# Edge stage of a graph layer on one core: 16-bit one-hots stored in interleaved pairs, addresses without a bit mask, 160 columns of zeros instead of 256

## The reference, cut to what matters

```python
def _conv(h, e, src, dst, Wn_l, bn_l, We_l, be_l, Wc_l, bc_l):
    hn = h @ Wn_l + bn_l
    et = e @ We_l + be_l
    m = hn[src] + et
    s = segment_sum(m, dst, num_segments=N_NODES)
    cnt = segment_sum(ones, dst, num_segments=N_NODES)
    agg = s / maximum(cnt, 1.0)[:, None]
    return concatenate([hn, agg], axis=1) @ Wc_l + bc_l
```

## Time and profile before

| | |
|---|---|
| time, median of 3 runs | 385.04 us (384.15 to 385.57) |
| profiled execution, span from first to last instruction | 380.0 us (the page gives no other time of it) |
| PE busy | 341.5 us, 90% |
| DVE busy | 248.8 us, 65% |
| granted TensorE clock, mean of the span | 0.982 |
| share of PE in the chain that ended last | 84% |

### The profile page before, as it was taken

How to read it: one execution, slowest core, us unless ns; L and a number is a source line. 1 busy time by engine, 2 the same in 40 slices (tenths; PEclk the granted TensorE clock), 3 DMA queues, 4 the chain that set the end, 5 groups by cost and what they waited for, 6 DMA issues and landing times.

```text
span 380.0 us, 9574 instructions
## 1 busy us (share of the span) xinstructions
PE 341.5 (90%) x2763; PEld 250.0 (66%) x2763; DVE 248.8 (65%) x659; ACT 150.1 (39%) x469; POOL 130.3 (34%) x243
## 2 busy tenths in 40 slices
PE   0599999999899999999989999999999999999910
PEld 0467777999688788886745566666666665567800
DVE  1647859993343425076798877769879998467640
ACT  1335536410121504113704466544556665444600
POOL 6200000600000000053670355456556666454536
PEclk9999999999999999999999999999999999999975
DMA  7941105830299930000061679999999999999005
GB/s 208 258 115 49 41 10 126 204 110 11 78 392 385 387 144 0 0 3 0 0 223 56 224 293 385 384 387 385 384 361 387 386 383 387 386 383 340 4 1 67
DMA packets 52456, 79.11 MB, mean 208 GB/s; under 512 B 3307, under 2 KB 19895, under 8 KB 52408
## 3 DMA queue, kind: packets, MB, share of 16 engines
q1 hardware_dynamic: 50458, 76.81, 58.2%
q0 software_dynamic: 720, 0.64, 1.5%
q10 hardware_dynamic: 1230, 1.05, 1.0%
HBM read 77.21 MB, written 1.30 MB: 207 GB/s over the span
## 4 chain that ended last, share of the span: by engine, by line
PE 84%; DVE 5%; DMA 3%; issue 2%; POOL 2%; ACT 1%; SPq 1%; POOLq 0%; DVEq 0%; ACTq 0%
PE ps L1280 82%; DMA reg<-in_L_gnn_Wc_dram 3%; PE ps L1283 3%; POOL out_dram L591 1%; DVE reg L1273 1%; DVE reg L910 1%; DVE cols L1142 0%; POOLq L105 0%; SPq L398 0%; DVE reg L1136 0%; DVE colp L1148 0%; ACT reg L620 0%; ACT reg_w L629 0%; POOL reg_w L580 0%; DVE acc L964 0%
## 5 line engine op out<-in xcount | busy, mean ns | idle before, releaser
L1280 PE MATMUL ps<-reg 128*64 128x256 f32 (+5 forms) x1399 | 237.9, 310 | 2.7 <-issue 1.1
L1280 PEld LDWEIGHTS ps<-reg 128*64 128x64 f32 (+5 forms) x1399 | 163.8, 143 | 17.4 <-issue 4.6
L1280 PE MATMUL ps<-reg,reg_w 128*64 (+1 forms) x688 | 154.9, 384 | 1.4 <-issue 1.3
L1280 PEld LDWEIGHTS ps<-reg,reg_w 128*64 128x64 f32 (+1 forms) x688 | 93.6, 138 | 50.6 <-issue 6.3
L580 POOL TENSOR_TENSOR reg_w<-reg_w 128x128 f32 x150 | 76.2, 508 | 78.4 <-ACT reg_w L811 59.9
L1228 DVE SCALAR_TENSOR_TENSOR reg_w<-reg_w,nid,reg 128x128 f32 x167 | 61.7, 373 | 24.9 <-PE ps L1280 19.2
L810 ACT COPY reg_w<-ps 64x128 f32<-64x128 f32 x150 | 39.3, 262 | 62.6 <-PE ps L1280 62.0
L1228 DVE SCALAR_TENSOR_TENSOR reg<-reg_w,reg 128x128 f32 x150 | 60.9, 406 | 0.4 <-issue 0.4
L1280 PE MATMUL ps<-zeros_b 128*128 128x256 bf16 (+1 forms) x231 | 53.5, 301 | 0.7 <-ACT reg L698 0.7
L811 ACT COPY reg_w<-ps 64x128 f32<-64x128 f32 x150 | 39.0, 260 | 3.7
L910 DVE TENSOR_TENSOR reg<-iota,idxH 125x660 bf16<-125x660 f16 (+5 forms) x42 | 38.8, 991 | 0.0
(11 more groups left out here) (252 smaller groups left out, 292.9 us busy)
## 6 DMA issues: line engine op xcount, KB each, us to landing
reg<-in_L_ffn_w2s_dram SPq DMA_DIRECT2D x127, 512.0 KB, 11.4
reg<-in_edge_attr_dram SPq DMA_DIRECT2D x13, 336.0 KB
reg<-in_L_gnn_Wc_dram SPq DMA_DIRECT2D x3, 512.0 KB, 9.7
reg<-in_L_gnn_Wn_dram SPq DMA_DIRECT2D x3, 256.0 KB, 5.9
reg<-in_x_dram ACTq DMA_DIRECT2D x1, 512.0 KB
out_dram<-acc SPq DMA_DIRECT2D x1, 512.0 KB
reg<-in_edge_attr_dram SPq DMA_DIRECT2D x13, 39.0 KB
reg<-in_L_mix_w_qkv_dram ACTq DMA_DIRECT2D x1, 384.0 KB, 7.0
```

What stands on the lines that cost most here:

```text
L1280: return e.matmul(to, lhsT, rhs, start=start, stop=stop, skip_group_check=True)
```

## The change

There are three edits in the edge stage.

The one-hots of 16 bits are stored in interleaved pairs. Before, `jhot` and `bhot` held one row per unit: index (block, half), then column. Now the index is block, column, half, so that the two halves of a block alternate element by element. VectorE compares `iota2`, a row in which each number stands twice (0, 0, 1, 1, ...), with the pair of keys of the two halves; the innermost two elements of all three operands are then neighbours in memory. Before, the innermost step of the keys was zero. POOL makes `iota2` once at the start. PE reads `bhot` and `jhot` of a half with a step of two elements (4 bytes). `dhot` stays as it was.

The low address is computed as word - (word >> 12) * 4096 instead of word & 4095. 

IDLE is 160 instead of 256.

```diff
-IDLE = 256
+IDLE = 160
-        bhot = part16(reg_q, 0, EP, BF16, HR * EG * 2, 128)
+        bhot = part16(reg_q, 0, EP, BF16, HR * EG, 128, 2)
-        jhot = part16(reg, 10958, EP, BF16, HR * EG * 2, JX + 1)
+        jhot = part16(reg, 10958, EP, BF16, HR * EG, JX, 2)
+        iota2 = part16(reg, 16000, 128, F16, 128, 2)
...
+            e.iota(iota2, [[1, 128], [0, 2]], base=0, channel_multiplier=0,
                    allow_small_or_imprecise_dtypes=True).then_inc(made, 1)
...
-                for to, w, j in ((jhot[:, s0:s0 + n, 0:JX], JX, 1), (dhot[:, s0:s0 + n, :], WX, 2), (bhot[:, s0:s0 + n, :], 128, 0)):
-                    keys = idxH[:, j, b:b + n // 2, :].rearrange("p b q -> p (b q)")
-                    ins = e.tensor_tensor(to, iota[0:EP, 0:w].unsqueeze(1).broadcast_to([EP, n, w]),
-                                          keys.unsqueeze(2).broadcast_to([EP, n, w]), ALU.is_equal)
+                def pairs(to, w, j):
+                    e_keys = idxH[:, j, b:b + n, :].unsqueeze(2).broadcast_to([EP, n, w, 2])
+                    return e.tensor_tensor(to, iota2[0:EP, 0:w, :].unsqueeze(1).broadcast_to([EP, n, w, 2]), e_keys,
+                                           ALU.is_equal)
+                pairs(jhot[:, s0:s0 + n, :, :], JX, 1)
+                keys = idxH[:, 2, b:b + n, :].rearrange("p b q -> p (b q)")
+                e.tensor_tensor(dhot[:, 2 * s0:2 * (s0 + n), :], iota[0:EP, 0:WX].unsqueeze(1).broadcast_to([EP, 2 * n, WX]),
+                                keys.unsqueeze(2).broadcast_to([EP, 2 * n, WX]), ALU.is_equal)
+                ins = pairs(bhot[:, s0:s0 + n, :, :], 128, 0)
...
-                    at_w, at_e = within(at[b % RU] & 4095, E_TAIL - JX), within(at[b % RU] >> 12, 4096 - WX)
+                    at_hi = at[b % RU] >> 12
+                    at_w, at_e = within(at[b % RU] - at_hi * 4096, E_TAIL - JX), within(at_hi, 4096 - WX)
...
-                        mm(ps_flat[:, bass.ds(at_w, JX)], bhot[:, s, :], jhot[:, s, 0:JX], False, False)
+                        mm(ps_flat[:, bass.ds(at_w, JX)], bhot[:, s, :, q], jhot[:, s, :, q], False, False)
```

More of the change, by code:

```diff
@@ L301, in graph_layer @@
         MADE = {n: i + 1 for i, n in enumerate((
-            "ident", "lhs", "e65", "ones", "thr", "iota", "below", "row0", "kk", "ones_b", "zeros_b", "bd",
+            "ident", "lhs", "e65", "ones", "thr", "iota", "iota2", "below", "row0", "kk", "ones_b", "zeros_b", "bd",
             "er_ones", "ids", "row65"))}
@@ L474, in _ @@
             e.iota(iota[:, :], [[1, R]], base=0, channel_multiplier=0,
+                   allow_small_or_imprecise_dtypes=True).then_inc(made, 1)
+            e.iota(iota2, [[1, 128], [0, 2]], base=0, channel_multiplier=0,
                    allow_small_or_imprecise_dtypes=True).then_inc(made, 1)
@@ L902, in edge_hots @@
                     e.wait_ge(idx_T, 1)
-                    e.wait_ge(made, MADE["iota"])
+                    e.wait_ge(made, MADE["iota2"])
                 if g >= HR:
                     e.wait_ge(edge_done, g - HR + 1)
-                b, n = g * EG, 2 * len(blocks(g))
-                s0 = g % HR * 2 * EG
-                for to, w, j in ((jhot[:, s0:s0 + n, 0:JX], JX, 1), (dhot[:, s0:s0 + n, :], WX, 2), (bhot[:, s0:s0 + n, :], 128, 0)):
-                    keys = idxH[:, j, b:b + n // 2, :].rearrange("p b q -> p (b q)")
-                    ins = e.tensor_tensor(to, iota[0:EP, 0:w].unsqueeze(1).broadcast_to([EP, n, w]),
-                                          keys.unsqueeze(2).broadcast_to([EP, n, w]), ALU.is_equal)
+                b, n = g * EG, len(blocks(g))
+                s0 = g % HR * EG
+                def pairs(to, w, j):
[7 more added lines that the diff above has]
+                ins = pairs(bhot[:, s0:s0 + n, :, :], 128, 0)
                 ins.then_inc(hots, 1)
@@ L1448, in _ @@
                     for q in range(2 if b < NB - 1 else 1):
-                        s = b % (HR * EG) * 2 + q
-                        mm(ps_flat[:, bass.ds(at_w, JX)], bhot[:, s, :], jhot[:, s, 0:JX], False, False)
+                        s = b % (HR * EG)
+                        mm(ps_flat[:, bass.ds(at_w, JX)], bhot[:, s, :, q], jhot[:, s, :, q], False, False)
                         mm(ps[:, 0, 0:IDLE], zeros_b[:, 0:128], zeros_b[:, 0:IDLE], False, False)
-                        ins = mm(ps_flat[0:EC, bass.ds(at_e, WX)], er[:, 2 * b + q, :], dhot[:, s, :], False, False)
+                        ins = mm(ps_flat[0:EC, bass.ds(at_e, WX)], er[:, 2 * b + q, :], dhot[:, 2 * s + q, :], False, False)
                 ins.then_inc(edge_done, 1)
```

## The result

The changed kernel is not faster: 388.15 us in the median of 16 runs (384.56 to 396.08), against 384.76 us for the kernel before in as many runs beside it (382.55 to 385.61). The ratio is 1.007, 95% interval 1.0045 to 1.0095. Forecast were 378.8 us, a range of 377.3 to 382.6 and 0.05 for slower: wrong in sign.

A forecast was written before the change was run, and what follows sets the result against it. Sequencer (5.74 to 5.8 us per 12 blocks) and array (5.4) were taken to bound the edge stage together. 385.0 - 6.2 (columns and mask together) - 0 (pairs, stepped operands) = 378.8 us, range 377.3 to 382.6.

The forecast's parts named there:

- What bounds the kernel: Edge stage: sequencer's beat of 5.74 to 5.8 us and array's 5.4 us per 12 blocks bound it at once.
- 160 columns: Edge stage on PE: 0.225 falls to 0.185 us per unit, 6.6 us if the sequencer kept pace.
- No mask: PE's sequencer, edge stage: one ALU_OP less, a five-step instruction of 90 ns; saves 75 ns per block.
- the sequencer's sum decides: Both edits together, edge stage: 83 blocks x 0.075 = 6.2 us off the stage.
- The rival of the dear instruction: Sequencer: long register instruction takes 135 ns, saving 30 ns per block, 2.5 us in all, 382.5 us; chance 0.10.
- The gap at the load: Array's gap at each table load in the edge stage: about as before, 0.34 to 0.46 us.
- The clock: Rival: with fewer zeros the granted clock drops to 0.50 in the edge stage, about 406 us; chance 0.05.
- two stretches of before: Against the clock's fall: 1.00 held with a 0.70 us pause, and at 45.5 to 48.9 with 25 records.
- Stepped operands on PE: Steps of two for `bhot` and `jhot`: put at 0; as a rival near 381 us, chance 0.14.
- the 27 ns: Upper bound per unit for stepped weight loads of `bhot` on PE, should they have doubled.
- Pairs on VectorE: Interleaved one-hots: compares of about 950 and 490 ns, worth 0 in time (bounds 0 and 0.3 us of gain).

The follow-up runs named there:

- two words, six blocks, 256 columns: Changed kernel with a block's two addresses as two table words, one load per six blocks, 256 columns of zeros: 383.04 us, ratio 0.9999.
- two-word run with 160 columns: Changed kernel with a block's two addresses as two table words, 24 words per load for 12 blocks: 397.7 us median, 382.94 to 405.56.

## Why the prediction was wrong

Step by step, by its own parts.

*What bounds the kernel* was read rightly: the sequencer's beat of 5.8 us and the array's 5.4 in one stage. With the array alone (constant addresses) the stage takes 30.6 us instead of 40, and with a short sequencer and the old array (two words, six blocks, 256 columns) 39.9.

*160 columns*: forecast 0.185 us per unit, measured 0.187 (0.186 with contiguous one-hots). Right as to the array; without the sequencer's part it bought next to nothing, as the prediction had said of either alone. That the weight load of `er` fits beneath 160 columns is right with it.

*No mask*: this is the step that failed, and within it a single term. Taken away was a mask of 32 + 60 ns; the records show 93 from its start to the next, so this was right. The instruction of five steps was put at 90 ns, after one of four steps with at most 87 in the tree stage; it takes 167. It lies outside the bounds, too: 135 was meant as the dearest case, each added step as dear as the shift. The other register instruction fell from 73 to 37. Lengths and what lies between them sum to 365 ns before and after (the 390 of the prediction are a mean that holds other waits as well), so the saving of 75 ns per block was 0, and the 6.2 us with it. By its own word ("the sequencer's sum decides") the forecast then stands at no change. The rival of the dear instruction named this cause, with a chance of 0.10, but priced it too low: it still left a gain of 2.5 us, and the gain was 0.

*The gap at the load*: forecast as before, 0.34 to 0.46, since both sides would shrink alike. With the sequencer at 0.365 us per block and the array at 0.374 there is no lead left to build. By the records a block's first register instruction starts 0.22 to 0.33 us ahead of its first product all the way to the last load, where before the distance grew from 0.19 us behind a load to between 0.75 and 0.92 ahead of the next. So nearly the whole load shows: 1.12 us from unit to unit, 0.94 beyond a unit, in place of 0.28 to 0.37. The last gap is longer in both kernels because the last load is: 1.33 us where the others take 0.85.

*The clock*: the rival on the other side, at 0.05, is what happened. Its condition was argued away by two stretches of before that had pauses and kept 1.00. One of them has a single pause of 0.70 us with 256 columns ahead of it; the changed kernel has five of 0.78 and then one of 1.25, with 160. The reasoning took for granted that the gaps stay small, and so rested on the failed step. That they would have stayed small, and the clock at 1.00, with the forecast 75 ns saved is argued and not shown; the nearest run is that with two words, six blocks per load and 160 columns, which keeps 1.00. The price, 406 us, was too high for the usual run since the clock fell only near the end of the stage. A unit at 0.50 takes 320 ns and not the 370 that doubling gives. In the two-word run with 160 columns, where it fell early, times up to 405.56 are there.

*How the loss divides*. The changed kernel's runs at 0.971 and 0.945 took 385.0 and 394.2 us, so 0.01 of mean clock is worth 3.5 us; carried to before's 0.982 that makes about 381, an estimate, below the 381.7 to 383.9 that the kernel before took at this mean clock. The edit of the columns thus gains perhaps 1 us (the last piece of the stage, which has no load behind it), and the clock takes 4 to 13.

*Stepped operands on PE*: 0, right. The unit with stepped one-hots is 187 ns, with contiguous ones 186; with 256 columns they are 227 and 225. That is at most 2 ns per unit, 0.3 us in the stage. Of the two rules of the Trainium skill that the prediction weighed, the note on cachelines in "SBUF — State Buffer" agrees with this also for the moving operand, for the step of two that was tried; the 27 ns that the prediction had drawn from the section on Fast Weight Load in "TensorE: Matmul & The Clock Gate" did not show.

*Pairs on VectorE*: forecast 950 and about 490 ns for the two compares, and no effect. Groups of DVE by form between 72 and 82 us after, in the columns of the earlier trace rows:

```profile
L914 DVE TENSOR_TENSOR reg<-reg,idxH 125x1536 bf16<-125x1536 f16 x4 | 3.8, 948 | 0.0
L914 DVE TENSOR_TENSOR reg<-reg,idxH 125x660 bf16<-125x660 f16 x3 | 1.5, 498 | 0.9 <-PE ps L1289 0.9
```

1744 became 948 and 833 became 498. The last compare starts at 80.7 us instead of 87.6, and the run with this edit alone has the time of before. Right in both.

## What to carry to other kernels

Where an engine's own sequencer is on the path, count register instructions by their measured length and by the 61 to 83 ns that each costs beside it, and measure a longer fused one before it is built on: here an extra word from memory was cheaper than three steps of arithmetic. A stage bound by two things needs both shortened, and shortening only the array turns its work into pauses. Columns of zeros that look like waste may be what keeps the clock, so take them away last, when the pauses are gone.

## What the runs showed of the hardware

- A fused register instruction on PE's sequencer took 37 or 42 ns with two steps, 73 with three (a shift among them), 83 to 87 with four in the tree stage, and 167 with the five of shift, multiply, subtract, multiply, add. Why the last is so dear is open: no run took the five steps apart.
- TENSOR_LOAD took 0.31 us for one word, 0.85 for 12, 1.11 for 16 and 1.62 for 24, so about 65 ns per word beyond the twelfth. The last load of the stage has fewer words and yet took longer: 1.33 us for 11 words and 1.10 for 10, which is why the last pause is the longest; the cause is open. PE's sequencer could be ahead of the array by 4.3 to 4.5 units and no more (0.98 us with 256 columns, 0.82 with 160, 1.45 with 160 at a clock of 0.50), so 12 words were nearly covered and 24 weren't.
- In the edge stage the clock fell only where 160 columns and long pauses came together: gaps of 0.78 us and then one of 1.25 to 1.32, or, in the run with 24-word loads, two gaps of 0.92 and 0.93 us (1.26 from unit to unit). It did not fall with 256 columns and gaps of 0.76 and 1.01, nor with 160 columns and gaps filled, nor with 160 columns and gaps of at most 0.39. Whether the pauses or the mean work of the array decide is open. In the profiled runs it stayed at 0.50 for 10.2 us (only the columns), 23.9 (the changed kernel) and 58.0 (two words, 160 columns).
- A single fall of 3.4 us outside the edge stage comes and goes without any change of the kernel. Of 82 runs of the kernel before, 45 had a mean clock of 0.981 to 0.983 and took 381.7 to 383.9 us, and 37 had 0.976 to 0.978, which is what the profiled runs with one such fall have, and took 383.9 to 386.1.
- A compare of 16-bit numbers whose three operands have neighbouring pairs took 948 ns for 1536 elements and 498 for 660, 0.51 ns per further element; with a key whose step is zero innermost it took 1744 and 833, 1.04 ns.
